# Graph attention on one core: the last of eight row slots read by one-hot matmuls in every group instead of every second one

## The reference

```
def _gatv2(x, src, dst, Wl, Wr, att, bias):
    xl = (x @ Wl).reshape(-1, H, C)          # H = 8 heads, C = 32
    xr = (x @ Wr).reshape(-1, H, C)
    e = leaky_relu(xl[src] + xr[dst], 0.2)
    logits = einsum('ehc,hc->eh', e, att)
    m = segment_max(logits, dst)
    p = exp(logits - m[dst])
    denom = segment_sum(p, dst)
    alpha = p / denom[dst]
    out = segment_sum(alpha[:, :, None] * xl[src], dst)
    return out.mean(axis=1) + bias
...
# three times: x = bn(leaky_relu(_gatv2(x, ...)) + x), the edges being the given ones and a self loop for each node
```

## Time and profile before

| what | value |
|---|---|
| time, median of 3 runs | 6016.44 us (6009.05 to 6019.91) |
| the profiled execution, from its first to its last instruction | 6035.8 us |
| TensorE busy, share of the span | 5102.4 us, 85% |
| TensorE weight loads | 3499.3 us, 58% |
| VectorE busy | 3709.3 us, 61% |
| ScalarE busy | 1751.6 us, 29% |
| GpSimd busy | 3865.9 us, 64% |
| the gathers of attention (L372) | 2340, 2247.6 us busy, 960 ns each |
| attention, layer 0 | from about 2582 us |
| attention, layers 1 and 2 | from about 3732 and 4882 us |

### The profile page before, as it was taken

How to read it: one execution, slowest core, us unless ns; L and a number is a source line. 1 busy time by engine, 2 the same in 40 slices (tenths; PEclk the granted TensorE clock), 3 DMA queues, 4 the chain that set the end, 5 groups by cost and what they waited for, 6 DMA issues and landing times.

```text
span 6035.8 us, 146385 instructions
## 1 busy us (share of the span) xinstructions
PE 5102.4 (85%) x51654; PEld 3499.3 (58%) x51654; DVE 3709.3 (61%) x7059; ACT 1751.6 (29%) x3755; POOL 3865.9 (64%) x4026
## 2 busy tenths in 40 slices
PE   4888888868886888769999995899999859999996
PEld 3666666668886888725555554455555535555554
DVE  6444444478788888746566556556566655656666
ACT  3222222245553000023333331333333223333331
POOL 3666666557774777567777761777777347777770
PEclk8888788879898999979999997899999979999998
DMA  4555455423332333234554442445444324444441
GB/s 103 138 137 137 132 147 138 131 73 88 86 87 69 95 93 97 67 89 123 125 128 123 123 115 57 104 125 125 125 123 125 95 59 124 124 122 124 123 125 56
DMA packets 689583, 661.13 MB, mean 110 GB/s; under 512 B 398676, under 2 KB 481051, under 8 KB 688859
## 3 DMA queue, kind: packets, MB, share of 16 engines
q1 hardware_dynamic: 555562, 484.42, 27.2%
q0 software_dynamic: 128960, 166.69, 15.1%
q10 hardware_dynamic: 4336, 0.67, 0.1%
HBM read 562.12 MB, written 89.17 MB: 108 GB/s over the span
## 4 chain that ended last, share of the span: by engine, by line
PE 63%; issue 16%; DVE 12%; POOL 5%; DVEq 3%; ACT 1%; ACTq 1%; DMA 1%; POOLq 0%
PE ps L1027 17%; PE ps L871 12%; PE ps L966 8%; POOL rows L372 5%; PE ps L987 4%; PE ps L835 4%; PE ps L818 3%; PE ps L1001 3%; PE ps L946 2%; PE ps L977 2%; PE ps L886 2%; PE ps L803 2%; PE ps L826 1%; DVE acc L1465 1%; DVE region L1452 1%
## 5 line engine op out<-in xcount | busy, mean ns | idle before, releaser
L372 POOL DMA_INDIRECT rows<-table,idx x2340 | 2247.6, 960 | 1120.4 <-issue 713.1
L1027 PE MATMUL ps<-region,hot 128*128 128x272 f32 x4992 | 1324.2, 409 | 190.1 <-DVE region L1702 84.7
L1027 PEld LDWEIGHTS ps<-region,hot 128*128 128x128 f32 x4992 | 916.4, 194 | 494.0 <-issue 293.1
L636 ACT ACTIVATE region<-ps 128x512 f32<-128x512 f32 x1248 | 677.3, 595 | 1680.9 <-PE ps L966 1680.9
L1734 DVE TENSOR_TENSOR acc<-acc,ps 128x272 f32 x1248 | 545.4, 437 | 891.4 <-PE ps L1027 775.4
L359 POOL DMA_INDIRECT rows<-table,idx x728 | 706.9, 971 | 432.8 <-PE ps L807 220.4
L871 PE MATMUL ps<-hot,region 128*128 128x192 bf16 (+1 forms) x8640 | 859.9, 260 | 63.9 <-DVE region L1568 56.7
L871 PEld LDWEIGHTS ps<-hot,region 128*128 128x128 bf16 x8640 | 785.1, 103 | 79.0 <-DVE region L1568 61.7
L1724 DVE TENSOR_TENSOR region<-ps,region 128x1056 f32<-128x1056 f32 x624 | 777.5, 1252 | 49.0 <-issue 44.8
L966 PE MATMUL ps<-xT,wcat 64*128 64x512 f32 x2496 | 714.6, 649 | 9.3 <-ACT region L636 9.3
L384 POOL DMA_INDIRECT rows<-table,idx x480 | 460.4, 959 | 242.4 <-issue 143.5
(11 more groups left out here) (302 smaller groups left out, 6765.3 us busy)
## 6 DMA issues: line engine op xcount, KB each, us to landing
hot<-hot_dram SPq DMA_DIRECT2D x624, 256.0 KB
turned<-turned_dram SPq DMA_DIRECT2D x624, 128.0 KB
rows<-table,idx POOLq DMA_INDIRECT x3548
hot_dram<-hot SPq DMA_DIRECT2D x104, 512.0 KB
region<-hot_dram SPq DMA_DIRECT2D x90, 512.0 KB
xwin<-table SPq DMA_DIRECT2D x1664, 24.0 KB
region<-d_dram SPq DMA_DIRECT2D x104, 256.0 KB
turned_dram<-turned SPq DMA_DIRECT2D x104, 256.0 KB
```

Of the source, the lines that this page charges most:

```text
L372: pool.indirect_dma_start(rows[:, n % 2, j, :], None, table, bass.IndirectOffsetOnAxis(ap=idx[:, s:s + 1], axis=0)).then_inc(rows_in3[n % ...
L636: act.activation(rz[g % 2][:, 2 * t + side, :], ps[:, Z + side, :], ACT.Relu).then_inc(rz_made, 1)
L1027: mm = pe.matmul(ps[:, AG + i, 0:PC + H], hot[:, b, 4 * side + 2 * i + j, :], px[b][:, 4 * side + 2 * i + j, :], start=(j == 0), stop=(j = ...
```

## The change

The last slot of every group, even ones too, is read on the core. GpSimd issues 7 gathers for each group, `rows_there` and ScalarE's copy count 7 slots, and `rows_in` takes slot 7 of every group from `xs` (a float32 matmul, L950 of before, for three bf16 ones) and waits for `one_kept` in each. `read_one` stands in every step, and so does `pick_one`; the counts of `one_read`, `one_picked` and `one_kept` follow. A `bt1` table now serves half a chunk (four groups), so there are 26 in a layer instead of 13, each from two small DMAs instead of one. Its four instructions are spread over the steps, one in each, ahead of the first `weigh`. `spanhot` has an entry for each group. Ahead of step 0 there are three reads and three picks instead of one.

The diff, cut to its core:

```diff
@@ rows_there, pool_attention
-            return rows_in3[n % 2], 16 * sum(8 - k % 2 for k in range(n % 2, n + 1, 2))
+            return rows_in3[n % 2], 16 * 7 * (n // 2 + 1)
...
-                for j, s in enumerate(piece_slots(g)[0:8 - g % 2]):
+                for j, s in enumerate(piece_slots(g)[0:7]):
@@ sp_attention
-                if u % 8 == 5:
-                    numbers_for(u // 8 + 2)
+                if u % 4 == 2:
+                    numbers_for((u + 10) // 4)
@@ rows_in
-                if g % 2 == 1:
-                    pe.wait_ge(one_kept, (l * G + g) // 2 + 1)
+                pe.wait_ge(one_kept, l * G + g + 1)
...
-                            if at < 7 or g % 2 == 0:
+                            if at < 7:
@@ read_one
-                at = l * CHUNKS + c
+                at = l * 2 * CHUNKS + g // 4
...
-                        mm = pe.matmul(ps[:, AG, 272:272 + cols], bt1[at % 2][:, k, m, :],
+                        mm = pe.matmul(ps[:, AG, 272:272 + cols], bt1[at % 2][:, k, 2 * (g % 2) + g % 4 // 2, :],
@@ pe_attention, the steps
+            read_one(0)
+            read_one(1)
             rows_in(0)
-            read_one(1)
+            read_one(2)
...
-                if u >= 8 and u % 2 == 0 and u + 3 < G:
+                if u >= 8 and u + 3 < G:
                     if k > 0:
                         pe.wait_ge(att_added, 4 * (l * G + k) - 1)
                     read_one(u + 3)
...
-                if u < 8 and u % 2 == 0:
+                if u < 8:
@@ attention on VectorE
                     def pick():
-                        if u % 2 == 0 and u + 3 < G:
+                        if u + 3 < G:
                             pick_one(l, u + 3)
-                    if phase in (3, 4) and u // 8 + 1 < CHUNKS:
-                        for q in range(2):
-                            stationary_one(l, u // 8 + 1, 2 * (phase - 3) + q)
+                    stationary_one(l, (u + 7) // 4, (u + 3) % 4)
```

More of the change, by code:

```diff
@@ L153, in build @@
         lane = sb("lane", [P, 1])
-        spanhot = sb("spanhot", [P, HALF, GROUPS], BF16)
+        spanhot = sb("spanhot", [P, G, GROUPS], BF16)
         fall = sb("fall", [H, 1])
@@ L498, in hot_for, with numbers_for @@
                                  hot_dram[8 * c + 4 * half + n // 2, :, at:at + 512]).then_inc(hot_in[b], 16)
-            def numbers_for(c):
-                if c >= CHUNKS:
+            def numbers_for(hc):
+                if hc >= 2 * CHUNKS:
                     return
-                at = l * CHUNKS + c
+                at = l * 2 * CHUNKS + hc
                 if at >= 2:
                     sp.wait_ge(bt1_made, FOLD * (at - 1))
[L506 to L509, removed]
+                last_of = r_dram.rearrange("a (f e) -> (a f) e", f=2).rearrange("(c t b m q) e -> c t b m q e", t=2, b=2, m=4, q=PIECE)
+                for b in range(2):
+                    sp.dma_start(rline1[at % 2].rearrange("p (b m e) -> p b m e", b=2, m=2)[:, b, :, :],
+                                 last_of[hc // 2, 1, b, 2 * (hc % 2):2 * (hc % 2) + 2, PIECE - 1, :].partition_broadcast(P)
+                                 ).then_inc(r1_in[at % 2], 16)
             numbers_for(0)
@@ L514, in sp_attention @@
             numbers_for(1)
+            numbers_for(2)
             for u in range(G + LAG):
-                if u % 8 == 5:
-                    numbers_for(u // 8 + 2)
+                if u % 4 == 2:
+                    numbers_for((u + 10) // 4)
                 if u + 2 < G:
@@ L623, in keep @@
                 act.wait_ge(*rows_there(l, g))
-                n = 8 - g % 2
-                act.activation(xs[:, (g // 8) % 2, g % 8, 0:n, 0:C], rows[:, (l * G + g) % 2, 0:n, 0:C], ACT.Copy).then_inc(xs_kept, 1)
+                act.activation(xs[:, (g // 8) % 2, g % 8, 0:7, 0:C], rows[:, (l * G + g) % 2, 0:7, 0:C], ACT.Copy).then_inc(xs_kept, 1)
             def turn(g):
@@ L991, in read_one @@
             def read_one(g):
-                c, m = g // 8, g % 8 // 2
-                at = l * CHUNKS + c
+                at = l * 2 * CHUNKS + g // 4
                 pe.wait_ge(bt1_made, FOLD * (at + 1))
-                if l * G + g > 1:
-                    pe.wait_ge(one_picked, (l * G + g) // 2)
+                if l * G + g > 0:
+                    pe.wait_ge(one_picked, l * G + g)
                 for k in range(FOLD):
@@ L1483, in prepare0 @@
                     c = n - 4
-                    ones_of = grp.rearrange("p (c a b m j) -> p c a b m j", c=CHUNKS, a=2, b=2, m=4)[:, :, 1, 1, :, PIECE - 1]
-                    tt(spanhot[:, 4 * c:4 * c + 4, :], wide(ones_of[:, c, :], GROUPS), down(iota[:, 0:GROUPS], 4), ALU.is_equal)
+                    ones_of = grp.rearrange("p (c a b m j) -> p c a b m j", c=CHUNKS, a=2, b=2, m=4)[:, c, 1, :, :, PIECE - 1]
+                    for b in range(2):
+                        tt(spanhot[:, 8 * c + b:8 * c + 8:2, :], wide(ones_of[:, b, :], GROUPS), down(iota[:, 0:GROUPS], 4),
+                           ALU.is_equal)
                 if n == 17:
@@ L1684, in _, with stationary_one @@
             layernorm(T1[:, :, :])
-            def stationary_one(l, c, k):
-                at = l * CHUNKS + c
+            def stationary_one(l, hc, k):
+                if hc >= 2 * CHUNKS:
+                    return
+                at = l * 2 * CHUNKS + hc
                 if k == 0:
-                    v.wait_ge(r1_in[at % 2], 16 * (at // 2 + 1))
+                    v.wait_ge(r1_in[at % 2], 32 * (at // 2 + 1))
                     if at >= 2:
@@ L1696, in pick_one @@
             def pick_one(l, g):
-                at = (l * G + g) // 2
+                at = l * G + g
                 v.wait_ge(one_read, at + 1)
@@ L1702, in pick_one @@
                 v.tensor_tensor(cand, ps[:, AG, 272:272 + GROUPS * C].rearrange("p (g c) -> p g c", g=GROUPS),
-                                wide(spanhot[:, g // 2, :], C), ALU.mult).then_inc(one_picked, 1)
+                                wide(spanhot[:, g, :], C), ALU.mult).then_inc(one_picked, 1)
                 v.wait_ge(one_picked, at + 1)
@@ L1840, in _ @@
                     stationary_one(l, 0, k)
-                pick_one(l, 1)
+                for g in range(3):
+                    pick_one(l, g)
+                for k in range(FOLD - 1):
+                    stationary_one(l, 1, k)
                 for i in range(8):
-                    if i in (3, 4):
-                        for k in range(2):
-                            stationary_one(l, 1, 2 * (i - 3) + k)
+                    stationary_one(l, (i + 7) // 4, (i + 3) % 4)
                     n = min(4, W - 4 * i)
```

14 lines of the change are left out of this document (6 added, 8 removed).

## The result

The changed kernel takes 6184.6 us (median of 4 runs, 6177 to 6192), the kernel before 6014.9 us (4 runs): a ratio of 1.029, with a 95% interval of 1.027 to 1.031. It is 170 us slower; the forecast was 152 us slower, 6168 us, with a range of 6112 to 6228.

A forecast was written before the change was run, and what follows sets the result against it. TensorE was taken to bound the middle of a layer, GpSimd the opening. Terms 45.9 + 6.1 + 3.9 + 1 - 6.3 = 50.6 us a layer, 152 us for three, gave 6168 us from 6016.4, range 6112 to 6228.

The forecast's parts named there:

- main step: Middle of a layer: TensorE sets the pace, not GpSimd, so gathers removed from step 10 on are worth nothing.
- The price of a read: TensorE, odd steps 11 to 99: 0.97 us per read plus 0.05 for the float32 matmul; 45 x 1.02 = 45.9 us a layer.
- Phase 1: Chunk ends with sums: second sums wait for the new pick, step 1.57 us longer; beyond the read, 11 x 0.55 = 6.1 us.
- The term for the second add and the pick: VectorE's path from `settle` at chunk ends: gap and second add 0.36 + 0.44 us, the pick's multiplication 0.38 us.
- the table instruction: VectorE's added table instruction, put at 0.39 us on the path from `settle` to TensorE's second sums.
- Phase 2: Step where TensorE already waits 2.7 us for the pick: a table instruction ahead of `weigh` adds 10 x 0.39 = 3.9 us.
- phase 0's 1 us: Table instruction ahead of the scans, mostly inside VectorE's wait for ScalarE: 0.1 us each, 1 us a layer.
- The opening: Start of each layer, steps without sums, GpSimd sets the pace: five fewer gathers and shorter wait at group 10, -6.3 us.
- The rule of the Trainium skill: VectorE in a two-port mode stops GpSimd writing DMA descriptors; in full, no opening gain and 6187 us; term left unchanged.
- GpSimd as the pace: Rival: GpSimd paces the groups, so 156 removed gathers give 1.25 us each, 195 us, 5821 us; chance 6%.
- VectorE as the pace of all odd steps: Rival: second sums wait for the pick in all odd steps, a read costs 1.57 us, 6224 us; chance 10%.
- Absorbed reads: Rival: new reads fall into TensorE's idle places; all 11 in phase 1 free gives 6117 us; within 0.2% chance 3%.

The follow-up runs named there:

- the two gather experiments: Kernel before without the eighth gather of even groups, no read added: 5990.0 us; changed kernel with that gather still issued, its rows unread: 6193.1 us.
- VectorE's new order: Kernel before, with VectorE serving TensorE first at a chunk's end (adds inside settle, pick ahead of scaling, adds ahead of weigh): 5924.0 us, ratio 0.986.
- the shorter reads: Changed kernel, each read multiplying with the high bf16 part of the table only, 4 matmuls instead of 12: 6027.7 us, ratio 1.003.

## Why the prediction was right

Its main step was to give the middle of a layer to TensorE, on the strength of one wait of 0.5 us against 97% of GpSimd's time. That held: 156 gathers taken away alone moved the middle by 0.1 to 2.0 us, as far as two profiles of the same kernel are apart, and given back alone they cost it 3.5 us of 960. Most of the signs named in advance came too: two steps take 18.80 us, GpSimd waits 122 us for buffers, its gathers with their issue (515 + 163 us) fill 85% of the stretch, and TensorE waits up to 3.2 us for the pick in phase 2 and 1.61 us in phase 1.

**The price of a read** was 1.02 us by the rows; two plain steps got 1.01 us longer. With 45 reads a layer this is 45.5 us of the 50.4.

**Phase 1** was put at 1.57 us over before and was 1.13. The term for the second add and the pick held: TensorE's second sums now start 1.68 us behind the start of the first add, against 0.54 us.

```profile
3017.76 0.44 DVE L1738 TENSOR_TENSOR acc<-acc,ps 128x272 f32 x1
3018.56 0.44 DVE L1738 TENSOR_TENSOR acc<-acc,ps 128x272 f32 x1 [0.36 <-DVE acc L1738]
3018.91 0.38 DVE L1707 TENSOR_TENSOR region<-ps,spanhot 128x224 f32<-128x224 f32 x1
...
3019.44 0.93 PE L1026 MATMUL ps<-region,hot 128*128 128x272 f32 x3 [1.61 <-DVE region L1707]
```

That is VectorE's two adds, the pick's multiplication, and TensorE behind it (the trace after, phase 1). What failed is the table instruction, put at its full length of 0.39 us. The row of before showed 0.69 us of idle time ahead of the first add, in which VectorE loads the window numbers, and I didn't ask whether the instruction would fit in there. It did, but for 0.10 us. **Phase 2** was put at 10 x 0.39 = 3.9 us; there are 11 such steps in a layer and not 10, and by the means each got 0.22 us longer, 2.4 us in all, though two profiles of one kernel differ by 0.16 in this phase. These two terms (11 x 0.44 and 1.5) and phase 0's 1 us (it was 0) are 7.3 us too much a layer; about 2 us came back in phase 3, 1.19 us longer instead of 1.02, which I had not priced. That is most of the way to the 6.5 us by which the middle fell short of the forecast.

**The opening** was the step that was wrong: 6.3 us were to go from steps 0 to 10, and they got 0.8 us longer. The gathers' gain is real. It is 3 to 4 us by the two gather experiments, and TensorE's waits for gathers in steps 0 to 9 fell from 23.8 to 16.9 us a layer. Some 3 us more came ahead of step 0 (69.1 to 65.9 us), since the first group is one gather shorter; my 6.3 us had that gather in them, at 1.25 us, and it gave more than its price. But the new pick of step 7 stands in VectorE's program ahead of the memset and the scans of the first chunk, and took the gain back: TensorE waits 3.9, 4.6 and 3.7 us for these scans in the three layers, which it did not before, and moving the memset ahead of the pick brought 4.4 us. I had asked of each new wait what TensorE does behind it, in the steps with sums. I didn't ask it of VectorE in the opening, though the pick was new there too.

The rule of the Trainium skill that I weighed against this gain (SBUF — State Buffer, SBUF: two separate sides) would have given 6187 us by my estimate, and the measured 6184.6 is nearer to that than to my 6168. That is a coincidence as far as the traces tell: in the openings a gather takes 0.96 us in the mean and the next one starts 1.25 us after it (median), in the changed kernel as in the one before, and with the memsets moved the opening ended 3.6 us below before's, with twice the picks and tables in it. No run tested the rule alone.

**How much of the number is luck.** The sum of a layer, 50.6 us, and the measured 50.4 + 0.8 = 51.2 agree because two errors of opposite sign cancel: the middle was put 6.5 us too dear and the opening 7.1 us too cheap. That they are so nearly equal is luck. Less the 3.2 us that came ahead of step 0 in each of layers 1 and 2, three layers make 147 us, which is the 146 us of the profiled spans. The other 24 us of the medians' difference are not in the parts of a layer. The profile of before was 19 us over its median, and the stages ahead of attention vary by more than that; that the rest lies there is likely and not shown, and the 13 instructions that I put at 0 are in there too.

**The rivals.** GpSimd as the pace is refuted in the kernel before, but it was close: 3.6 us less on TensorE per chunk, with VectorE's new order, was more than enough to make it true. VectorE as the pace of all odd steps is refuted by the plain steps, in which no wait for the pick appears; it does rule the steps that end a chunk, as the shorter reads showed. Absorbed reads are refuted by the same plain steps, each 1.01 to 1.02 us longer; only in phase 1 is a part of the read hidden.

## What to carry to other kernels

Where two engines look full, ask which one is waited for; here the 97% of GpSimd's time was worth next to nothing while TensorE hardly ever waited for it, and moving its work to TensorE cost the full price in every plain step. When work is added to an engine's program, look behind it in that same program: a wait that is harmless in itself may stand ahead of a long instruction (here a 5.7 us memset) that was on time until then. And before work is moved between engines, look for places where the bounding engine waits for a neighbour that could serve it first: that was worth 90 us here, where the move lost 170.

## What the runs showed that I had not expected

The stages ahead of attention took between 2561 and 2607 us in ten profiles, with the same code but for 13 short instructions, and the higher the granted clock of the first pass (0.83 to 0.87), the shorter they were on the whole. In the two profiles of the kernel before it was 0.84 and 0.87, and the second was the shorter by 38 us. In the middle of a layer of attention the six layers of these two profiles agree within 4 us of 910 (906.2 to 909.8).
